# First key-side rows of an attention loaded in one set of transfers, and two chunks' projections moved from ahead of the attention into its first units

## The reference, cut to what matters

```python
def _layer(x, c, wmod, attn, ffn):
    sa, ca, ga, sb, cb, gb = (silu(c) @ wmod).reshape(6, -1)
    ga = (2 * (ga >= 0) - 1) * maximum(abs(ga), 0.25)      # gb likewise
    h = layernorm(x) * (1 + ca) + sa
    x = x + ga * attn(h)
    h = layernorm(x) * (1 + cb) + sb
    return x + gb * ffn(h)

S = einsum('hid,hjd->hij', K, Q) * SCALE                   # layer 0
S = where(delta < 0, -inf, S) + decay                      # delta = i - j, decay = -delta
attn = einsum('hij,hjd->hid', softmax(S), V)
```

## Time and profile before

| | us |
|---|---|
| median of 3 runs | 1556.82 (1551.09 to 1563.71) |
| profiled execution, device time | 1552.29 |
| its span, first to last instruction | 1550.6 |
| TensorE busy in it | 1404.3 (91%) |
| VectorE busy in it | 1199.2 (77%) |
| ScalarE busy in it | 1038.3 (67%) |

### The profile page before, as it was taken

How to read it: one execution, slowest core, us unless ns; L and a number is a source line. 1 busy time by engine, 2 the same in 40 slices (tenths; PEclk the granted TensorE clock), 3 DMA queues, 4 the chain that set the end, 5 groups by cost and what they waited for, 6 DMA issues and landing times.

```text
span 1550.6 us, 35254 instructions
## 1 busy us (share of the span) xinstructions
PE 1404.3 (91%) x13320; PEld 593.6 (38%) x13320; DVE 1199.2 (77%) x1592; ACT 1038.3 (67%) x2052; POOL 316.9 (20%) x376
## 2 busy tenths in 40 slices
PE   7887888899899999986899999999999989999998
PEld 5543333333333254442233333333333333236665
DVE  5678797898786044888899979997999779816766
ACT  2245575777688833231798978998988879984443
POOL 2401132000000033223500018200400040046225
PEclk9989999999999999996899999999999999999999
DMA  7621121111000003222200200000000000012455
GB/s 227 128 56 41 50 67 34 31 28 49 5 2 2 1 15 65 53 48 51 93 7 7 54 6 7 7 7 7 7 7 7 7 2 2 2 62 84 142 152 149
DMA packets 57611, 68.54 MB, mean 44 GB/s; under 512 B 10563, under 2 KB 53123, under 8 KB 56707
## 3 DMA queue, kind: packets, MB, share of 16 engines
q1 hardware_dynamic: 54379, 57.90, 14.1%
q0 software_dynamic: 3072, 8.39, 1.8%
HBM read 45.29 MB, written 26.74 MB: 46 GB/s over the span
## 4 chain that ended last, share of the span: by engine, by line
issue 40%; PE 32%; DVE 11%; POOL 8%; ACT 4%; DMA 3%; SPq 2%; POOLq 0%; DVEq 0%; ACTq 0%
DVE mpart L1747 8%; PE psum L1235 7%; PE psum L1210 4%; PE psum L1278 3%; PE psum L1179 3%; ACT probs L1482 3%; PE psum L1287 3%; PE psum L1306 3%; PE psum L1352 2%; PE psum L1371 1%; POOL ffn_w L953 1%; PE psum L1139 1%; DMA key_region<-in_w_up 1%; POOL key_region L965 1%; SPq L803 1%
## 5 line engine op out<-in xcount | busy, mean ns | idle before, releaser
L1747 DVE TENSOR_REDUCE mpart<-psum 128x2 f32<-128x1024 f32 (+2 forms) x832 | 913.7, 1155 | 101.4 <-PE psum L1179 84.3
L1482 ACT ACTIVATE probs<-psum 128x512 f32<-128x512 f32 (+3 forms) x1664 | 846.1, 573 | 172.1 <-PE psum L1210 94.9
L1235 PE MATMUL psum<-probs,v_region 128*17 128x256 f32 (+2 forms) x6144 | 495.2, 395 | 11.6 <-ACT out_sb L1497 7.9
L1179 PE MATMUL psum<-key_region,row_region 50*128 50x512 f16 (+3 forms) x1664 | 320.8, 378 | 65.9 <-DVE mpart L1747 50.6
L1210 PE MATMUL psum<-row_region,key_region 52*128 52x512 f16 (+3 forms) x1664 | 349.7, 378 | 15.7 <-ACT probs L1482 12.9
L1210 PEld LDWEIGHTS psum<-row_region,key_region 52*128 52x128 f16 x1664 | 97.8, 93 | 352.9 <-ACT probs L1482 292.1
L1235 PEld LDWEIGHTS psum<-probs,v_region 128*17 128x17 f32 x6144 | 102.7, 95 | 205.1 <-issue 101.1
L1179 PEld LDWEIGHTS psum<-key_region,row_region 50*128 50x128 f16 x1664 | 94.5, 93 | 167.5 <-DVE mpart L1747 98.1
L909 POOL TENSOR_SCALAR vare<-mv 128x4 f32<-128x4 f32 x16 | 3.7, 230 | 637.1 <-DVE mv L1661 637.1
L1517 ACT ACTIVATE probs<-psum,gate_s 128x512 f32<-128x512 f32 (+1 forms) x24 | 16.4, 682 | 69.8 <-PE psum L1278 69.8
L1018 POOL TENSOR_TENSOR key_region<-probs,key_region 128x512 f16<-128x512 f32 (+1 forms) x24 | 27.9, 1164 | 155.4 <-ACT key_region L1526 155.3
(11 more groups left out here) (191 smaller groups left out, 1329.2 us busy)
## 6 DMA issues: line engine op xcount, KB each, us to landing
parts<-key_region SPq DMA_DIRECT2D x32, 256.0 KB, 2.6
key_region<-parts SPq DMA_DIRECT2D x48, 128.0 KB, 4.5
row_region<-parts SPq DMA_DIRECT2D x192, 32.0 KB
sorted_x<-in_zero SPq DMA_DIRECT2D x46, 128.0 KB, 2.6
key_region<-sorted_x SPq DMA_DIRECT2D x46, 128.0 KB, 2.3
sorted_y<-key_region SPq DMA_DIRECT2D x46, 128.0 KB
key_region<-in_wmod SPq DMA_DIRECT2D x2, 1536.0 KB, 11.4
x_sb<-in_x SPq DMA_DIRECT2D x4, 512.0 KB, 8.7
```

The source lines that it names most:

```text
L1179: mm = pe.matmul(bank(b + par)[:, 0:w], rows[at, g, hp, r * P:(r + 1) * P], keys[at, g * HP + hp, q * CH:q * CH + w], start=True, stop=not ...
L1235: mm = pe.matmul(psum[32 * h:32 * h + VW, SUM_BANK, lo:hi], v_sb[:, jt, g * HG + h, :], probs[:, (S0[y] + s) % 2, h, lo:hi], start=(jt == ...
L1482: nc.scalar.activation(probs[:, (S0[y] + s) % 2, 2 * hp + par, off:CH], psum[:, e % 3, off:CH], ACT.Exp, scale=SCALES[y]).then_inc(s_p, 1)
L1747: V.tensor_reduce(mpart[:, n % NG, at:at + 2, q:q + 1], psum[:, b:b + 2, 0:w], AX.X, ALU.max).then_inc(drained(*item)[0], 1)
```

## The change

1. Layer 0's and layer 1's chunk-0 rows, for all four groups of heads, come by one `rows y 0`: 6 transfers of 128 KB instead of four times 6 of 32 KB, and 2 of constants instead of 8; layer 0's 2 constants are issued at the kernel's start. They have a semaphore of their own (`s_rows`), for which every block of units 0 to 3 waits in full.
2. The prologue keeps the projections of chunks 0 and 1 only. Those of chunks 2 and 3, layer 1's gates (`mg`, `gates`) and `mr` go into the steps of units 0 to 3 (`with_projections`), each at the end of a step, with what VectorE does for it (`ql`, `va`, `gates`, `ra`) behind the first block of the next step. Layer 0's gates come later in the prologue.
3. `block_share` gives the steps of units 0 to 2 of layer 0 a share of 0.6: through step 15 the attention now has 41 blocks instead of 42, and 5, 4, 3, 3 instead of 5, 3, 3, 3 in steps 16 to 19; from step 18 on the walk is the same.
4. `csb` and `gtmp` lie in the end of `ffn_w`, the exponential's wait for the gates is gone, and the unused constant `identb` is no longer loaded.

```diff
+def block_share(y, n, k):
+    if y:
+        return CHUNK_END.get(k, 1) if n and n % NG == 0 else 1
+    return 0.6 if n < NG - 1 else 1
...
-    out += [("st", 0, 3), ("rows", 0, 0), ("rows", 0, 1), ("rows", 0, 2), ("rows", 0, 3)]
...
+    out += [("v", 0, 0), ("nm", 0, 2), ("va", 0, 0), ("st", 0, 3), ("qk", 0, 1, 0), ("ql", 0, 1, 0), ("ln", 0, 2), ("lh", 0, 2), ("nm", 0, 3)]
+    out += [("qk", 0, 1, 1), ("ql", 0, 1, 1), early.pop(0), early.pop(0), ("ln", 0, 3), ("lh", 0, 3), early.pop(0), early.pop(0)]
...
+def with_projections(items):
+    after = {(0, 0): [("qk", 0, 2, 0)], (0, 2): [("qk", 0, 2, 1)], (1, 0): [("v", 0, 2)], (1, 1): [("keys", 0, 2)], (1, 2): [("mg", 1)],
+             (1, 3): [("qk", 0, 3, 0)], (2, 1): [("qk", 0, 3, 1)], (2, 2): [("v", 0, 3)], (3, 0): [("keys", 0, 3)], (3, 1): [("mr",)]}
...
-        prob_words = probs[:, :, :, :].rearrange("p b h t -> p (b h t)")
-        csb = prob_words[:, 0:2 * KD * P].rearrange("p (k n) -> p k n", k=2 * KD)
+        first_end = ffn_w[:, 0, KD * F0:]
+        csb = first_end[:, 0:2 * KD * P].rearrange("p (k n) -> p k n", k=2 * KD)
...
         def rows_loaded(y, n):
-            i = n // NG
-            return 128 * (i + 1) if y == 0 else 128 * NCH + 128 + 96 * i
+            i, g = n // NG, n % NG
+            if i == 0:
+                return s_rows, 128 * (y + 1)
+            return s_row[g], 128 * i if y == 0 else 128 * (NCH - 1) + 96 * i
...
+            def load_first_rows(y):
+                sp.wait_ge(*parts_stored(y, 0, 0))
+                if y:
+                    first_row_constants(y)
+                for par in range(2):
+                    for k, part in enumerate(ROW_PARTS):
+                        src = parts[0, part, :, 0:CH].rearrange("(h r c) t -> r c h t", r=2, c=HD)[par]
+                        lo = 64 * par + C0 + HD * k
+                        sp.dma_start(rows[lo:lo + HD, :, :, :].rearrange("p g h t -> p (g h) t"), src).then_inc(s_rows, 16)
...
-                if s == 0 and y == 0 and hp == 0:
-                    act.wait_ge(s_mod, NLAY)
```

More of the change, by code:

```diff
@@ L271, in project_rows @@
         if p == 0:
-            out.extend([("rows", 1, n) for n in range(NG)])
+            out.append(("rows", 1, 0))
     for tc in range(1, NCH):
@@ L380, in prologue_walk @@
-    out += [("mc", 1), ("mg", 1), ("mr",), ("wo", 0), ("xb", 0, 0), ("xb", 0, 1), ("xb", 0, 2)]
-    for it in (("qk", 0, 2, 0), ("ql", 0, 2, 0), ("ln", 0, 3), ("lh", 0, 3), ("xb", 0, 3), ("qk", 0, 2, 1), ("ql", 0, 2, 1), ("keys", 0, 2), ("v", 0, 2)):
-        out += [it] + [early.pop(0) for _ in range(2 * (it[0] in ("ql", "lh", "v")))]
-    out += [("mp", 0, 0), ("gates", 1), ("qk", 0, 3, 0), ("ql", 0, 3, 0), early.pop(0), early.pop(0), ("mt", 0, 0), ("place", 0, 0)]
-    out += [("qk", 0, 3, 1), ("ql", 0, 3, 1), ("keys", 0, 3), early.pop(0), early.pop(0), ("v", 0, 3)]
@@ L853, in _ @@
                     load_keys(*it[1:])
+                elif it[0] == "rows" and it[2] == 0:
+                    load_first_rows(it[1])
                 elif it[0] == "rows":
@@ L1911, in _ @@
                     low_parts(("qk", *it[1:]))
-                elif it[0] == "v":
-                    value(it)
+                elif it[0] == "va" or it[0] == "v" and it[1]:
+                    value(("v", *it[1:]))
                 elif it[0] == "max":
```

69 lines of the change are left out of this document (42 added, 27 removed).

## The result

The changed kernel is slower: 1581.89 us median (1575.84 to 1586.8, 4 runs) against 1557.57 us (1551.09 to 1563.71, 4 runs) for the kernel before beside it, a ratio of 1.0139 with a 95% interval of 1.0103 to 1.0175. (The quotient of the two medians is 1.0156. The recorded ratios, which this document uses throughout, can differ from such quotients by up to 0.002.) The forecast was 1556.3, the range 1545 to 1568. The profiled execution has a span of 1576.2 us against 1550.6. That difference of 25.6 us is a little more than the ratio's 21.7, at least in part because the execution of the kernel before that was profiled is one of its quicker ones (1552.29 us, where later groups of runs of the same kernel have medians of about 1561).

The account below looks back on a forecast made before the run. TensorE, busy 91% of the span, was taken as the bound. Prologue +5.3, units -2.2, clock -0.7, layer 1 +2.4 make +4.8, less 0.8: +4.0 on 1552.29 gives 1556.3 us, range 1545 to 1568.

Parts of the forecast that it names:

- the allowance at `mt`: First stage: 0.8 us taken off the sum for VectorE's wait at `mt`, partly given back in the first steps.
- The book's end: Unit 4's first step, put at 160.50 us before the change: TensorE's 126.69 busy plus 33.81 idle.
- 161 to 163: Sign of the forecast: unit 4's first step in the changed kernel would stand at 161 to 163 us.
- The last mark: Last sign of the forecast: from unit 4 on, distances as before.
- Prologue, idle, +5.3: Up to the first score: TensorE idle 26.3 us against 20.95, including 8.4 waiting for the merged rows.
- Rival D: Layer 0's and layer 1's first rows: wide transfers land quickly, at 43.4; -3.8 us, 1548.5; chance 0.13.
- The first score at 69 to 70: End of the prologue: the attention's first score would come at 69 to 70 us instead of 86.26.
- Units 0 to 3, idle, -2.2: Layer 0's units 0 to 3: TensorE idle 10.7 us against 12.86, VectorE catching up during projections.
- rival C: Units 0 to 3: with two slots, projections block later blocks; idle +8.4, total +14.6 us, 1567; chance 0.17.
- Clock, -0.7: Up to unit 4: one low-clock bout spared (-2.4), longer prologue gap costs +1.7; bounds -6 and +4.
- Blocks, 0: Smaller share: one of 42 blocks passes beyond step 15, -0.5 us, and comes back in step 17.
- Layer 1, +2.4: Layer 1's first block: merged rows land later, at 613.7 instead of 611.35 us; at most 3.5.

Follow-up runs that it names:

- spread pair: Changed kernel, gap before first block filled, layer 1's rows per unit: pieces spread over units 0 to 2 (spread kernel, 1.0046) against between first-stage blocks (0.9896).
- The pairs of runs: Moved pieces in the units against in the first stage: changed kernel 1.0139 against pieces grouped 1.0048; with the gap filled, 1.0046 against 0.9896.
- the second pair: The spread pair: gap filled, pieces spread over the units 1.0046, against pieces between the first stage's blocks 0.9896.
- all four pairs of runs: Small against full share: changed kernel 1.0139, 1.0151; kernel before 0.9943 against itself; merged rows added 0.9914, 0.9958; candidate 0.9896, 0.9925.
- The candidate: Changed kernel with the gap before the first block filled, later pieces between first-stage blocks, layer 1's rows per unit, small share: 0.9881, again 0.9896.
- the kernel with the gap filled: Changed kernel with chunk 1's values, layer 0's gates' product and layer 1's modulation columns put ahead of the first block: 1.0077.

## Why the prediction was wrong

The step that failed is the idle time of units 0 to 3: it was put at -2.2 us and measured +6.8. The next largest miss is the clock, put at -0.7 and measured +5.4. By its own terms up to unit 4's first step the prediction had 5.3 - 2.2 - 0.7 - 0.8 = +1.6, and the runs' +20.5 exceeds that by 18.9: 9.0 from the units, 6.1 from the clock, 3.0 from the prologue, 0.8 from the allowance at `mt`. By its own steps:

- **The book's end.** The first step of unit 4 was put at 160.50 us, read off the wrong step; it is 139.00. The forecast for units 0 to 3 so rested on a window that held 21.5 us of unit 4. The changed kernel has this step at 159.51. Read against the 161 to 163 that was to show the forecast true, that looks like a near hit, and it is luck: against the right row it is +20.5. The last mark, "from unit 4 on, distances as before", held (+21.4 at unit 3, +20.3 at unit 15).
- **Prologue, idle, +5.3.** Right in kind, short in size: +8.3. The first block came at 50.76 after 10.15 us, where 48.8 and 8.4 stood. Rival D is out. Mis-sized were the landing of the rows, which came out at my upper bound ("if the stores of chunk 1 mix with them, 51"; they are issued from 42.34, but that they did the delaying isn't shown), and the wait at the gates' slot, 3.02 us, for which I had 1.7 at `mt`. The other terms came out close: 10.40, 2.11, 0.43 and 2.89 us where 10.5, 2.0, 0.7 and 3.0 stood. "The first score at 69 to 70": 76.58, of which 3.0 us are this idle time and 4.0 the clock. ScalarE's 15.66 us wait is gone, as said, and bought nothing that shows in the changed kernel. On rival D the prediction let the trace say that the merged total is quicker but the first quarter later. No trace of merged rows existed then; the runs show it now, with the first block at 50.76 against 47.08 for rows per unit.
- **Units 0 to 3, idle, -2.2.** This is the step that failed, in two ways. It took 5 us off for the time that a projection gives VectorE to catch up in. VectorE and TensorE were about equally loaded there (41.85 and 43.46 of 52.74 us), and with two slots VectorE has at most two slots' worth of blocks to work off before it waits for TensorE (4.97 us around the piece shown). And the sum itself was wrong. It took the 2.43 us of the entry off the 12.86 as "already counted above", but the window starts at 86.26, behind that wait, so the 12.86 never held them. Its own terms, -5 and +5.2, give +0.2, so the gain of 2.2 comes from this subtraction alone. Measured is +6.8. In the spread pair it is 1.3 us for each of eight pieces, and no catching up shows. This was rival C's direction and near its size, +8.4, with its slots (7.6 us of waits for pieces' copies); C's 1567 fell short because the clock and the prologue had the forecast's terms.
- **What the pieces left behind.** The sum had no term for it: "work that is moved behind the first blocks" was taken as cover for the queue alone. It was also the cover for the blocks' maxima in the first stage. The pairs of runs price presence in the units and absence in the first stage together at 14 us with the gap and 23 us without it; in the second pair's profiles 3.8 us of it are idle time of the first stage.
- **Clock, -0.7.** It is +5.4 in busy time, outside my bounds of -6 and +4. Some 4.0 of it lie in the first stage, where the stretch after the long gap ran at 0.70; the clock in the units, 0.89, is nearly that of before, 0.90.
- **Blocks, 0.** The statement counted only blocks beyond step 15 and missed that the steps of unit 3 take 12 blocks where 9 stood (units 0 to 3: 10, 10, 9, 12 against 12, 11, 10, 9). Priced, the share is a small gain: in all four pairs of runs the small share was the faster, by 0.1 to 0.6%, clear of no change on the kernel before and just so with the merged rows added, but not in the other two. Why it gains stays open.
- **Layer 1, +2.4.** 7.16 us of idle instead of 3.42, +3.7, just over my "at most 3.5"; with what follows, some 5 us by the profiles and 0.4% by the ratios.

A chain of runs leads from the kernel before to the changed one, at 1561 us to the unit. Merged rows of layer 0: -6.6 us (0.9958). The small share on top: -6.9 (0.9914). The candidate's order with the full share instead: +1.7 (0.9925). The early first block with its gap, and the later pieces in one group behind the blocks instead of between them: +14.4 (1.0017); in the profiles all of this lies in the first stage, 9.5 us of idle time and 5.0 of busy time. Layer 1's rows merged, and the small share: +4.8 (1.0048). The pieces in the units: +14.2 (1.0139). Each kernel is compared with the next, so the sum is the 21.7 us of the ratio 1.0139 by construction and proves nothing. Each term is uncertain by 5 to 7 us, so the two of +14 are clear of noise, the first two just, and the other two are not.

## What to carry to other kernels

Two kinds of work that load two engines in opposite proportion can hide each other where they alternate. Before moving one away, price what it leaves bare as well as what it displaces. In a stage whose pipeline is two slots deep, an inserted piece can stall two engines one after the other: the next one while the piece runs, and this one while the piece is copied out. It cost 1.3 us of idle time for each piece here, and several pieces side by side hid each other's copies. Merging small transfers gained on the queue and lost for the first consumer here, so look at what stands between the load and that consumer. And when a book is cut at a time, check that the row at the cut is the step that it is said to be, and that no wait is counted on both sides.

## What the runs showed of the hardware

The granted clock also fell with no long gap ahead. In the kernel with the gap filled, TensorE ran 10 us at 0.50 in unit 5. It was busy for 9.22 of them, with no idle time over 0.8 us in the rows of that stretch; the idle times just ahead of it were 1.16 us at 185.69 and 0.70 at 188.04. Its windows:

```profile
185.00:190.00 5.00, 3.62 (x35) 1.50 (x37) 2.39 (x3) 4.32 (x12) 2.27 (x2) 0.81 0.13 39
190.00:195.00 5.00, 4.47 (x26) 0.89 (x22) 3.60 (x7) 3.02 (x6) 0.00 (x0) 0.50 0.14 33
195.00:200.00 5.00, 4.75 (x34) 1.96 (x38) 2.83 (x6) 1.78 (x5) 0.00 (x0) 0.50 0.15 33
```

The clock dips at this place of the work in other kernels too, but for less long. A clock of 0.81 over 5 us is 1.9 us at the lower level. Added up in this way over the windows there, the time at that level is 3.4 us in the kernel before (175 to 185 us), the changed one (200 to 205) and the spread one (190 to 200), and 13.6 in this one. Units 4 to 7 took it 4.2 us longer than the changed kernel. The spread kernel has the same filled gap and doesn't show this, so it isn't what the filled gap brings with it, and what makes the dip long wasn't tried.

The executions of one program differ in the same way. Those of the kernel before with the small share run from 1551.44 us at a mean clock of 0.976 to 1560.71 at 0.968. In the latter, which was profiled, the stretch from 60 to 70 us had a clock of 0.66 where the profile of the kernel before, with the same first stage, had 0.83.
